# One block of 128 columns for a chunk's router weights, and one output-bias product for two tiles

## The reference

```python
feat = jnp.mean(x, axis=0)
w = jax.nn.softmax(feat @ Wr + br, axis=-1)
h = jax.nn.relu(_bn(jnp.einsum('bfd,edh->bfeh', x, W1) + b1, ...))
h = jax.nn.relu(_bn(jnp.einsum('bfeh,ehk->bfek', h, W2) + b2, ...))
y = jnp.einsum('bfeh,ehd->bfed', h, Wo) + bo
return jnp.einsum('bfed,fe->bfd', y, w)
```

## Time and profile before

| | us |
|---|---|
| median of 3 runs | 1150.87 (1149.9 to 1151.51) |
| profiled execution | 1151.33 |
| its span, first to last instruction | 1149.5 |
| PE busy | 1112.8 (97%) |
| DVE busy | 774.2 (67%) |
| ACT busy | 718.6 (63%) |
| POOL busy | 233.2 (20%) |
| mean granted TensorE clock | 0.977 |

### The profile page before, as it was taken

The page is one execution under the profiler, slowest core; times in us unless marked ns, Lnnn a source line. Parts: engine busy times, 40 slices in busy tenths (PEclk is TensorE's granted clock), DMA queues, the critical chain, the costliest instruction groups (busy, mean ns, idle before and its releaser), DMA issues. The chain is left out here.

```text
span 1149.5 us, 19520 instructions
## 1 busy us (share of the span) xinstructions
PE 1112.8 (97%) x6682; PEld 995.7 (87%) x6682; DVE 774.2 (67%) x1932; ACT 718.6 (63%) x1221; POOL 233.2 (20%) x272
## 2 busy tenths in 40 slices
PE   7799996899999999999999999999999999999998
PEld 5689995888988888889888888888888888888997
DVE  5688864657658667586586675865857758667564
ACT  3478762656566665665666656656566566566665
POOL 2487762230300301103003021030030200200000
PEclk9899996989999999999999999999999999999999
DMA  4598973011101111011001110111011101100000
GB/s 129 140 254 242 269 185 88 21 56 28 56 1 38 56 38 42 15 37 57 17 21 57 37 47 11 37 57 35 21 39 37 52 6 33 41 20 1 1 19 14
DMA packets 78472, 67.73 MB, mean 59 GB/s; under 512 B 27916, under 2 KB 73750, under 8 KB 78374
## 3 DMA queue, kind: packets, MB, share of 16 engines
q1 hardware_dynamic: 74101, 59.62, 18.6%
q0 software_dynamic: 3968, 6.61, 2.2%
q10 hardware_dynamic: 304, 0.26, 0.1%
HBM read 40.66 MB, written 25.80 MB: 58 GB/s over the span
## 5 line engine op out<-in xcount | busy, mean ns | idle before, releaser
L1207 DVE SCALAR_TENSOR_TENSOR accumulated<-bank,router_w,accumulated 128x256 f32<-128x256 f32 (+2 forms) x392 | 169.5, 479 | 212.7 <-PE bank L264 199.2
L551 ACT ACTIVATE h<-weight_stage 128x512 fp32r<-128x512 f32 (+2 forms) x208 | 114.5, 598 | 187.9 <-PE bank L264 166.4
L262 PE MATMUL bank<-ffn_w_high,h 128*128 128x256 f32 (+2 forms) x784 | 221.5, 282 | 2.2 <-DVE h L1028 1.7
L264 PE MATMUL bank<-ffn_w_high,h 128*128 128x256 f32 (+2 forms) x784 | 221.9, 283 | 1.5 <-issue 1.5
L263 PE MATMUL bank<-ffn_w_low,h 128*128 128x256 f32 (+2 forms) x784 | 221.6, 283 | 0.0
L675 ACT ACTIVATE weight_stage<-bank,bn_cols 128x512 f32<-128x512 f32 (+2 forms) x208 | 155.5, 752 | 74.3 <-PE bank L264 61.7
L675 ACT ACTIVATE activated<-bank,bn_cols 128x512 f32<-128x512 f32 (+2 forms) x208 | 156.8, 754 | 61.4 <-PE bank L264 54.6
L1028 DVE TENSOR_TENSOR h_low<-activated,h_high 128x512 fp32r<-128x512 f32 (+2 forms) x209 | 135.0, 657 | 79.4 <-ACT h_high L551 78.2
L262 PE MATMUL bank<-xT_high,ffn_w_high 128*128 128x512 f32 (+2 forms) x416 | 161.7, 389 | 0.0
L262 PE MATMUL bank<-h_high,ffn_w_high 128*128 128x512 f32 (+2 forms) x416 | 158.2, 380 | 1.6 <-DVE h_low L1028 1.3
L263 PE MATMUL bank<-xT_low,ffn_w_high 128*128 128x512 f32 (+2 forms) x416 | 158.9, 382 | 0.0
(11 more groups left out here) (194 smaller groups left out, 1949.2 us busy)
## 6 DMA issues: line engine op xcount, KB each, us to landing
x_rows<-in_x SPq DMA_DIRECT2D x18, 512.0 KB, 5.2
x_turned<-xT_high SPq DMA_DIRECT2D x22, 256.0 KB, 4.9
x_turned<-xT_low SPq DMA_DIRECT2D x22, 256.0 KB, 6.5
mix_xT_high<-x_turned SPq DMA_DIRECT2D x11, 512.0 KB, 3.6
mix_xT_low<-x_turned SPq DMA_DIRECT2D x11, 512.0 KB, 4.5
out<-accumulated SPq DMA_DIRECT2D x11, 512.0 KB, 3.4
weight_stage<-in_L_ffn_W SPq DMA_DIRECT2D x16, 256.0 KB, 5.0
node_table<-gathered SPq DMA_DIRECT2D x22, 130.0 KB, 4.4
```

What stands on the lines that cost most here:

```text
L262: nc.tensor.matmul(dst, ah, bh, start=(k == 0 and not lead), stop=False)
L264: last = nc.tensor.matmul(dst, al, bh, start=False, stop=(k == n - 1))
L551: return nc.scalar.activation(dst, src, ACT.Copy)
L1207: last = V.scalar_tensor_tensor(a, Yb[b][0:tp, (t % 2) * D:(t % 2 + 1) * D], wts(ch)[0:tp, t, e:e + 1], a, ALU.mult, ALU.add)
```

## The change

The router weights of a chunk lie in one block: w3 becomes 128 partitions x 4 tiles x 32 columns (Q = 32) in place of 4 x 128. One turn of 128 columns gives a w3T of 128 x 128, in which tile t's 24 rows stand at partition 32 t. bo3 becomes a block diagonal of 128 x 4 x 256: tile t's bias rows at partitions 32 t, in the columns of tile t, zero elsewhere. The product of w3T with the columns of two tiles is then one instruction of 512 columns. router_turned copies 128 columns instead of up to 512.

The set-up of bo3 is made anew: bo is loaded into all 128 partitions (bo_raw, in the place that w1m has in `accumulated`), split by bo_parts behind tile 5 and put into the blocks by bo_rows, eight copies behind tile 9. mid_blocks moves to tile 7 and bn_fold to tile 12. w1m's load moves to tile 24, w1_sums from tile 15 to 35, its eviction from 16 to 36, bias_cols from 17 to 37. turn_bn stays behind tile 14.

```diff
-        bo3 = sb("bo_rows", [P, D], f32r)
+        bo3 = sb("bo_rows", [P, TPC, D], f32r)
-        w3T = sb("router_wT", [P, TPC, P], f32r)
-        w3 = sb("router_w3", [P, TPC, P])
+        w3T = sb("router_wT", [P, P], f32r)
+        w3 = sb("router_w3", [P, TPC, Q])
+        bo_raw, bo_low = accf[:, KT * 3 * D:KT * 3 * D + D], accf[:, KT * 3 * D + D:KT * 4 * D]
...
-        SETUP_Q, SETUP_POOL, SETUP_BN = 2, 8, 12
-        LD_SMALL = 27
+        SETUP_Q, SETUP_ROUTER, SETUP_POOL, SETUP_BN = 2, 4, 16, 20
+        LD_SMALL = 24
...
-            sp.dma_start(w1m, I["L0_mix_w1"].rearrange("(k p) n -> p k n", p=P)).then_inc(s["ld_small"], 16)
-            for r in range(3):
-                sp.dma_start(w3[r * NE:(r + 1) * NE, 0:2, :].rearrange("p a b -> p (a b)"), I["L0_ffn_bo"]).then_inc(s["ld_small"], 16)
+            sp.dma_start(bo_raw,
+                         I["L0_ffn_bo"].unsqueeze(0).broadcast_to([P // NE, NE, D])).then_inc(s["ld_small"], 16)
...
                 if i == NTILES // 2:
                     load_turned(CHUNKS[0])
+                    need(sp, s["set_pool"], SETUP_POOL)
+                    sp.dma_start(w1m, I["L0_mix_w1"].rearrange("(k p) n -> p k n", p=P)).then_inc(s["ld_w1m"], 16)
...
+            def bo_parts():
+
+                pch.step(nc.gpsimd.tensor_copy(bo3[:, 0, :], bo_raw))
+                pch.step(low(bo_low, bo_raw, bo3[:, 0, :]))
+                pch.step(nc.gpsimd.memset(bo3[:, :, :].bitcast(fp32), 0.0))
+                pch.step(nc.gpsimd.memset(w3[:, :, :], 0.0))
 
             def bo_rows():
-                bo = w3[:, 0:2, :].rearrange("p a b -> p (a b)")
-                bo_low = w3[0:3 * NE, 2:4, :].rearrange("p a b -> p (a b)")
-                nc.gpsimd.memset(bo3[:, :].bitcast(fp32), 0.0).then_inc(s["ones"], 1)
-                pool.wait_ge(s["ones"], 3)
-                pch.step(nc.gpsimd.tensor_copy(bo3[0:3 * NE, :], bo[0:3 * NE, :]))
-                pch.step(low(bo_low, bo[0:3 * NE, :], bo3[0:3 * NE, :]))
-                pch.step(nc.gpsimd.tensor_copy(bo3[0:3 * NE, :], bo_low))
-                pch.step(nc.gpsimd.tensor_copy(bo3[0:2 * NE, :], bo[0:2 * NE, :]))
+
+                for t in range(TPC):
+                    pch.step(nc.gpsimd.tensor_copy(bo3[t * Q:(t + 1) * Q, t, :], bo_low[t * Q:(t + 1) * Q, :]))
+                for t in range(TPC):
+                    half = slice(t * Q, t * Q + 2 * NE)
+                    pch.step(nc.gpsimd.tensor_copy(bo3[half, t, :], bo_raw[half, :]))
                 assert pch.n == SETUP_POOL
-                nc.gpsimd.memset(w3[:, :, :], 0.0).then_inc(s["ones"], 1)
...
-            CHORES = {3: router_w, 4: bo_rows, 6: mid_blocks, 10: bn_fold, NTILES - 4: rstd_plus_one}
+            CHORES = {3: router_w, 5: bo_parts, 7: mid_blocks, 9: bo_rows, 12: bn_fold, NTILES - 4: rstd_plus_one}
...
-            CHORES = {2: g_high, 3: wq_evict, 8: bn_sqrt, 15: bn_evict, 16: w1_evict}
+            CHORES = {2: g_high, 3: wq_evict, 8: bn_sqrt, 15: bn_evict, 36: w1_evict}
...
-                copy(w3T[:, 0:nt, 0:tp], Fb[1][:, 0:nt * P].rearrange("p (t r) -> p t r", r=P)[:, :, 0:tp]).then_inc(s["fw3c"], 1)
+                copy(w3T[0:w, 0:tp], Fb[1][0:w, 0:tp]).then_inc(s["fw3c"], 1)
...
-                pe.wait_ge(s["ld_small"], 16 * LD_SMALL)
-                pe.wait_ge(s["xte"], 10)
+                pe.wait_ge(s["ld_w1m"], 16)
+                pe.wait_ge(s["xte"], 30)
...
-            CHORES = {2: turn_wq, 14: turn_bn, 15: w1_sums}
+            CHORES = {2: turn_wq, 14: turn_bn, 35: w1_sums}
...
-                for t in range(ch.nt):
-                    last = nc.tensor.transpose(Fb[1][:, t * P:t * P + tp], w3[0:tp, t, :], ident[0:tp, 0:tp])
-                last.then_inc(s["fw3T"], 1)
+                nc.tensor.transpose(Fb[1][0:w, 0:tp], w3[0:tp, 0:ch.nt, :].rearrange("p t q -> p (t q)"),
+                                    ident[0:tp, 0:tp]).then_inc(s["fw3T"], 1)
...
-                    for t in pair:
-                        last = nc.tensor.matmul(Fb[b][0:tp, (t % 2) * D:(t % 2 + 1) * D], w3T[:, t, 0:tp], bo3[:, :],
-                                                start=True, stop=True)
-                    last.then_inc(s["fbo"], 1)
+                    t0, t1 = pair[0], pair[-1] + 1
+                    nc.tensor.matmul(Fb[b][0:tp, 0:(t1 - t0) * D], w3T[0:w, 0:tp],
+                                     bo3[0:w, t0:t1, :].rearrange("p t d -> p (t d)"), start=True, stop=True).then_inc(s["fbo"], 1)
...
-            CHORES = {0: g_mean_off, 2: g_sums, 3: g_low, 9: bn_recip, 17: bias_cols}
+            CHORES = {0: g_mean_off, 2: g_sums, 3: g_low, 9: bn_recip, 37: bias_cols}
```

More of the change, by code:

```diff
@@ L21 @@
 NE = 8
+Q = 32
 NG = 2 * NH
@@ L198, in build @@
         L1b, L2b, Yb, Fb = bank[0:2], bank[2:4], bank[4:6], bank[6:8]
-        names = """ld_b ld_w0 ld_w1 ld_g ld_bn ld_small id ones eps set_pool w_sum bias_row kv_w kv_mean kv_w2 kv_hi kv_lo
+        names = """ld_b ld_w0 ld_w1 ld_g ld_bn ld_w1m ld_small id ones eps set_pool w_sum bias_row kv_w kv_mean kv_w2 kv_hi kv_lo
             g_mean g_w g_prod g_sum g_hi g_lo
@@ L462, in router_w @@
                 pch.step(low(wr2[:, :, NE:2 * NE], rl[:, 0:KT, :], wr2[:, :, 0:NE]))
-            def bo_rows():
-                bo = w3[:, 0:2, :].rearrange("p a b -> p (a b)")
-                bo_low = w3[0:3 * NE, 2:4, :].rearrange("p a b -> p (a b)")
-                nc.gpsimd.memset(bo3[:, :].bitcast(fp32), 0.0).then_inc(s["ones"], 1)
-                pool.wait_ge(s["ones"], 3)
-                pch.step(nc.gpsimd.tensor_copy(bo3[0:3 * NE, :], bo[0:3 * NE, :]))
-                pch.step(low(bo_low, bo[0:3 * NE, :], bo3[0:3 * NE, :]))
-                pch.step(nc.gpsimd.tensor_copy(bo3[0:3 * NE, :], bo_low))
-                pch.step(nc.gpsimd.tensor_copy(bo3[0:2 * NE, :], bo[0:2 * NE, :]))
+                assert pch.n == SETUP_ROUTER
+            def bo_parts():
[3 more added lines that the diff above has]
+                pch.step(nc.gpsimd.memset(w3[:, :, :], 0.0))
+            def bo_rows():
+                for t in range(TPC):
[3 more added lines that the diff above has]
+                    pch.step(nc.gpsimd.tensor_copy(bo3[half, t, :], bo_raw[half, :]))
                 assert pch.n == SETUP_POOL
-                nc.gpsimd.memset(w3[:, :, :], 0.0).then_inc(s["ones"], 1)
             def mid_blocks():
@@ L481, in mid_blocks @@
                 nc.gpsimd.memset(bk2, 0.0).then_inc(s["ones"], 1)
-                pool.wait_ge(s["ones"], 6)
+                pool.wait_ge(s["ones"], 4)
                 for h in range(P // HC):
@@ L730, in router_turned @@
             def router_turned(ch):
-                tp, nt = ch.tp, ch.nt
+                tp, w = ch.tp, ch.nt * Q
                 need(act, s["fw3T"], ch.c + 1)
                 need(act, s["fbo"], ch.b0)
-                copy(w3T[:, 0:nt, 0:tp], Fb[1][:, 0:nt * P].rearrange("p (t r) -> p t r", r=P)[:, :, 0:tp]).then_inc(s["fw3c"], 1)
+                copy(w3T[0:w, 0:tp], Fb[1][0:w, 0:tp]).then_inc(s["fw3c"], 1)
             FRONT = {1: gnn_exp, 2: gelu, 5: x2_high, 6: router_exp}
@@ L840, in x_table @@
                     need(pe, s["bn_ev"], 1)
-                if g == 13:
+                if g == 33:
                     need(pe, s["w1_ev"], 1)
@@ L976, in router_turn @@
             def router_turn(ch):
-                tp = ch.tp
+                tp, w = ch.tp, ch.nt * Q
                 need(pe, s["fw3"], ch.c + 1)
-                for t in range(ch.nt):
-                    last = nc.tensor.transpose(Fb[1][:, t * P:t * P + tp], w3[0:tp, t, :], ident[0:tp, 0:tp])
-                last.then_inc(s["fw3T"], 1)
+                nc.tensor.transpose(Fb[1][0:w, 0:tp], w3[0:tp, 0:ch.nt, :].rearrange("p t q -> p (t q)"),
+                                    ident[0:tp, 0:tp]).then_inc(s["fw3T"], 1)
             def out_bias(ch):
@@ L985, in out_bias @@
                 need(pe, s["fw3c"], ch.c + 1)
+                w = ch.nt * Q
                 for b, pair in enumerate(ch.pairs()):
-                    for t in pair:
-                        last = nc.tensor.matmul(Fb[b][0:tp, (t % 2) * D:(t % 2 + 1) * D], w3T[:, t, 0:tp], bo3[:, :],
-                                                start=True, stop=True)
-                    last.then_inc(s["fbo"], 1)
+                    t0, t1 = pair[0], pair[-1] + 1
+                    nc.tensor.matmul(Fb[b][0:tp, 0:(t1 - t0) * D], w3T[0:w, 0:tp],
+                                     bo3[0:w, t0:t1, :].rearrange("p t d -> p (t d)"), start=True, stop=True).then_inc(s["fbo"], 1)
             FRONT = {2: mix1, 3: mix2, 5: x2_turn, 6: router}
```

## The result

| kernel | median us (runs) | ratio to before, 95% |
|---|---|---|
| before | 1150.57 (1149.44 to 1151.53, 7 runs) | |
| after | 1154.69 (1151.29 to 1157.04, 7 runs) | 1.0033 (1.0018 to 1.0047) |

The account below looks back on a forecast made before the run. TensorE was taken as the bound, in the main loop and after tile 11 of the node phase. Main loop -4.2, wait for bn_fold +7.1, clock +1.7 give +4.6 us: 1155.5 us, range 1150.5 to 1159.0.

Parts of the forecast that it names:

- the start: GpSimd's sum for tile 5, from which its queue was added up, taken to begin at 51.78 us as before.
- the clock's 1.7 us: Half clock on TensorE after its idling at turn_bn: one dip, +1.7 us, with 0 and 3.4 as ends.
- at TensorE's pace: Node phase after tile 11 runs at TensorE's speed, 2.79 us a tile, so a stop there is not caught up.
- Turns and bias products: TensorE in the main loop: one turn for four saves 3.96 us, wide bias products 0.2, together -4.2 us.
- The copy, the moved w1 steps: ScalarE's shorter copy of turned weights and w1_sums, its eviction and bias_cols moved by 20 tiles: zero.
- moved and merged loads: w1m's load moved to tile 24 and three bias loads made one, on SP: zero.
- The queue on GpSimd: Set-up work ahead of bn_fold takes 27.6 us from tile 5's sum, so turn_bn starts near 79.4: +7.1 us.
- The node phase in all: Tiles 0 to 48: the stop at turn_bn and the clock's dip together, +8.8 us.
- (a): Rival: GpSimd's backlog doesn't reach bn_fold, which waits only for tile 12; stop 3.7 us, 1150.4 to 1152.1; chance 0.15.
- (b): Rival: the stop at tile 14 is absorbed, only the main loop's gain counts, 1146.7 us; chance 0.07.
- (c): Rival: two clock dips, or longer ones near 180 to 257 us, 1157.2 to 1158.9 us; chance 0.13.
- (d): Rival: the wide product or wide turn costs what it replaces, 1159.7 us; chance 0.05.

Follow-up runs that it names:

- e10: The changed kernel, unchanged, timed again beside the kernel before: 1153.58 us, ratio 1.0038 to before.
- e6: The changed kernel with 24 unread products of 128 columns on TensorE ahead of turn_bn's wait: 1142.89 us, ratio 1.0033 to before.
- e2: The changed kernel with turn_bn moved on TensorE from tile 14 to 20, GpSimd's queue as changed: 1149.38 us, ratio 0.9989 to before.
- e12: The changed kernel with turn_bn in tile 20 and job 2's split ahead of bo_rows in tile 9: 1148.47 us, ratio 0.9997 to before.
- e7: The changed kernel with the block turned four times instead of once in a full chunk: 1145.06 us, one execution.
- e8: The changed kernel with the bias product made tile by tile, 256 columns each: 1141.27 us, one execution.
- e1: The changed kernel with nothing edited, run for a second trace: 1153.3 us beside 1150.3, one execution.
- e3: The changed kernel with bn_fold back behind tile 10 and bo_rows behind tile 12: 1148.53 us, ratio 0.9982 to before.
- e9: The kernel before, unchanged, run for its trace: 1149.78 us median.
- e4: The kernel before with only bn_fold moved from tile 10 to 12: 1154.07 us, ratio 1.0035 to before.
- e5: The changed kernel with mid_blocks and bn_fold at tiles 6 and 10, bias set-up spread to tiles 16, 19 and 22: 1135.09 us, ratio 0.9970 to before.
- e11: The changed kernel with its GpSimd set-up spread, the kernel of e5 on another chip: 1147.02 us, ratio 0.9976 to before.

## Why the prediction was right, and where it was off

The forecast was 1155.5 us, +4.6. The median is 1154.69 us, +4.1 in that comparison and +3.8 in e10's. The mechanism was right: a gain in every chunk, and a larger loss because TensorE waits for bn_fold behind the new work on GpSimd. That the number came so close is in part luck: the start was off by 1.3 us, the clock's 1.7 us are not seen at the end of the phase, and some of what the median loses is in no trace (below).

**What bounds the kernel.** Right for the main loop: 0.38 us off TensorE in a chunk came off the span in each. For the node phase "at TensorE's pace" was too simple: e6 gave TensorE 1.94 us that were gone again by S 48, and e2 and e12 lose 3.4 to 4.2 us with no wait at turn_bn.

**Turns and bias products.** -3.96 and -0.2, together 4.2. A single turn has 0.12 us now, e7 gives 0.33 for three and e8 0.05 for the bias products, where 0.02 was taken. Eleven periods gave 4.16 (3.85 by the forecast's terms), the end 0.23. The rates of the Trainium skill, "TensorE: Matmul & The Clock Gate", section "Back-to-back issue gap", would have made the chunk 0.46 us shorter, and it is 0.38. Its saving of 0.22 on the bias products is not there, since 512 columns still take 0.23 and not 0.131; its 0.24 for three turns is less than the 0.33 of e7.

**The copy, the moved w1 steps.** Nothing, as forecast: ScalarE's copy is under 0.3 us, and w1_sums' 0.9 us left S 12 to S 15 and stand further on. Of the moved and merged loads the prediction said zero as well. The nine traces of kernels that are alike up to there (after, e1, e2, e3, e6, e7, e8, e10, e12) have S 9 at 60.56 to 65.83 us, seven of them at 63.2 to 64.6; the three of before, e9 and e4 have it at 64.95 to 65.43. A gain of some 1 us at the start may be there; it is not shown, and was not tested alone.

**The queue on GpSimd.** Right in kind and nearly in size. From the sum of tile 5 to the end of bn_fold it took 77.71 - 50.45 = 27.26 us, against 27.6 worked out; bo_parts 54.26 - 51.68 = 2.58 against 2.59, bo_rows 69.09 - 65.40 = 3.69 against 3.76. turn_bn stood at 77.76 and not at 79.4, as the sum of tile 5 began at 50.45 instead of 51.78. The delay of turn_bn was therefore +5.4 us in the trace's own time, not +7.1; counted from S 9 it is 77.76 - 64.12 - (72.37 - 65.43) = 6.7. The start, held fixed in the working, is the term that was off. Why it came earlier is open.

**The clock.** One dip of 1.7 us was added, and 1.94 is what it costs where it stands. At S 48 no trace shows that price: without the dip (e6) the way there from the turn is as long as with it (e7, e8). So this step, that the dip's length adds to the time, failed as far as one trace of each can tell. The rows of ScalarE fit loads that set the pace behind the dip and take up its price there. The median can't decide: the forecast misses it by 0.8 us with the 1.7, and by 0.9 without.

**The node phase in all**: +8.8 by the forecast; S 48 comes 7.75, 7.01 and 6.05 us later in the three traces. Less the main loop's 4.4 that leaves 1.7 to 3.4 us, and the medians say 4.1 and 3.8. Two of the three traces are of the fastest execution of their set, so where the median ones lose the rest can't be placed.

**The rivals.** (a) is false for the change: the backlog reached bn_fold, and turn_bn stood at 77.76, not at 76.0. Its premise, bn_fold bound by tile 12 alone, has its own experiment in e4: the stop is 2.48 us and not 3.7, yet the time is 3.8 us longer, between the 3.7 that (a) had for the stop alone and the 5.4 with a dip. (b), the stop absorbed, is false as a whole, and may hold for the part of the dip. (c) is not seen: one dip follows the stop, and none of the ten bridges traced on these chips is longer than before's 88.50 us; executions that were not traced can't be told. (d) is false by e7 and e8.

**What is not settled.** Without any stop, but with the set-up in tiles 5 to 12, the phase from S 9 to S 48 is 2.8 to 4.2 us longer than before (e2, e3, e12); spread to tiles 16 to 22 it is 0.7 to 2.0 longer (e5 and e11, against either trace of before). e12 excludes job 2's split as the one cause. Whether it is the loads behind the splits, the shifts for ScalarE or the sums that free VectorE's buffers was not separated; all three stand in one queue.

## What to carry to other kernels

A step that is moved back in an engine's queue has to be followed to its consumer, and the consumer moved with it or the step put ahead of the new work: here a set-up in the wrong order let the node phase end 6 to 8 us late, more than the 4.4 that the change had gained. Moving the consumer alone (e2) takes away the wait and not the backlog; putting the new work where the queue has room (e5, e11) takes away nearly all. Price the queue from one row per operation, add it up to the step that is awaited, and start from where the queue last waited. Saved time on one engine counts only up to the next resource that runs near its limit; ahead of a stretch with the DMA engines busy for 0.97 of the time, 1.9 us of TensorE left no trace at the end of the phase.

## What the runs showed of the hardware

GpSimd's casts of 256 columns cost 0.40 us on 128 partitions, and four of them start to end take 1.77 us on 32 partitions and 1.78 us on 16: between 16 and 128 partitions the price goes by columns.

The kernel before takes 1150 us on two of the chips and 1138 on a third. The spread version was traced on two of them: 1147.02 us in e11 and 1134.87 in e5, with the same code. The difference lies around chunk 0: from its turn to that of chunk 1 it takes 54.10 us in e11 and 44.60 in e5. ScalarE in order of time, in e11, has idle times there that e5 doesn't show:

```profile
213.13 0.99 ACT L685 ACTIVATE weight_stage<-bank,bn_cols 128x240 f32<-128x240 f32 x2 [1.73 <-remote]
...
246.78 0.60 ACT L561 ACTIVATE xT_high<-bank 128x512 fp32r<-128x512 f32 x1 [2.29 <-remote]
```

What releases it ("remote") is not in the trace. These 12 us are three times what the change is about, so times were compared on one chip only.
